# Another order of stages inside one step of a conv-mixer and mixture-of-experts kernel

## The reference, cut to what matters

```python
gating, index = jax.lax.top_k(affinity, k)
x_in = jnp.take_along_axis(x[:, None, :, :], index[..., None], axis=2)
h = jax.nn.gelu(jnp.einsum('bekd,edh->bekh', x_in, w1) + b1[None, :, None, :])
x_e = jnp.einsum('bekh,ehd->bekd', h, w2) + b2[None, :, None, :]
out = out.at[jnp.arange(Bx)[:, None], idx_flat].add(vals_flat)
```

## Time and profile before

| | us |
|---|---|
| median of three executions | 2999.71 |
| lowest, highest | 2988.85, 3001.3 |
| the profiled execution, its own time | 3005.34 |
| span of its instructions | 3002.5 |
| PE busy in it | 2067.5 (69%) |
| DVE busy | 1884.6 (63%) |
| ACT busy | 1360.2 (45%) |
| POOL busy | 1953.0 (65%) |

### The profile page before, as it was taken

One profiled execution on the slowest core, in us unless ns is written; L12 is line 12 of the kernel. 1 busy time (PEld: TensorE's weight loads), 2 busy tenths in 40 slices (PEclk: granted clock), 3 DMA queues, 4 the chain that ended last, 5 costly groups with the idle time before them and its releaser, 6 DMA issues.

```text
span 3002.5 us, 38138 instructions
## 1 busy us (share of the span) xinstructions
PE 2067.5 (69%) x11080; PEld 1164.1 (39%) x11080; DVE 1884.6 (63%) x4664; ACT 1360.2 (45%) x2308; POOL 1953.0 (65%) x1551
## 2 busy tenths in 40 slices
PE   3676777767777678777777777777777878744342
PEld 1233334343434344444434343444434443433221
DVE  1467686768677675858586776758675876753000
ACT  1334354554546454545545464545545364523210
POOL 0000256868777767778686767777686777777774
PEclk8877689898889887888889898888888797955555
DMA  4030415362534426263625435262625353334332
GB/s 114 10 81 0 115 22 131 46 148 36 119 76 93 106 44 147 42 152 46 148 35 119 74 76 117 44 152 44 149 41 135 51 107 73 71 63 79 40 61 50
DMA packets 284643, 244.66 MB, mean 81 GB/s; under 512 B 52368, under 2 KB 251264, under 8 KB 282112
## 3 DMA queue, kind: packets, MB, share of 16 engines
q0 software_dynamic: 110592, 80.31, 21.0%
q1 hardware_dynamic: 173824, 161.62, 18.7%
HBM read 83.71 MB, written 99.09 MB: 61 GB/s over the span
## 4 chain that ended last, share of the span: by engine, by line
PE 27%; issue 19%; POOL 16%; DVE 13%; ACT 10%; DMA 8%; SPq 6%; POOLq 0%; DVEq 0%; ACTq 0%
PE psum L1381 12%; POOL acc_dram L913 11%; POOL G L899 5%; PE psum L1407 5%; SPq L827 4%; DMA acc_dram<-Y,IDA 4%; DMA G<-rows_dram,IDX 3%; PE psum L1574 2%; ACT RS L935 2%; PE psum L1565 2%; PE psum L1417 2%; DVE hots L1277 2%; DVE XS L1189 2%; ACT RS L938 1%; PE psum L1487 1%
## 5 line engine op out<-in xcount | busy, mean ns | idle before, releaser
L913 POOL DMA_INDIRECT acc_dram<-Y,IDA x768 | 1163.2, 1515 | 446.0 <-issue 280.8
L899 POOL DMA_INDIRECT G<-rows_dram,IDX x768 | 784.2, 1021 | 578.5 <-issue 543.6
L1368 DVE TENSOR_TENSOR Y<-psum,GT 96x384 f32<-96x384 f32 x256 | 140.8, 550 | 450.4 <-PE psum L1574 390.4
L1277 DVE TENSOR_SCALAR_CACHE_REDUCE hots<-A,cand 96x384 f32<-96x384 f32 x720 | 401.6, 605 | 21.0 <-ACT A L1024 14.6
L1558 PE MATMUL psum<-m_all,G 96*128 96x96 f32 x768 | 130.9, 286 | 277.8 <-DMA G<-rows_dram,IDX 246.6
L1040 ACT ACTIVATE XG<-psum 128x288 f32<-128x288 f32 x256 | 103.7, 405 | 481.4 <-PE psum L1558 480.1
L1381 PE MATMUL psum<-U,m_all 128*128 128x384 f32 x576 | 266.9, 611 | 37.7 <-DVE DH L1133 28.0
L1574 PE MATMUL psum<-w2s,PH 128*96 128x128 f32 x1536 | 260.0, 316 | 0.0
L1381 PE MATMUL psum<-SQ,m_all 128*128 128x384 f32 x576 | 242.3, 549 | 20.3 <-DVE DU L1157 12.3
L1574 PEld LDWEIGHTS psum<-w2s,PH 128*96 128x96 f32 x1536 | 244.4, 198 | 14.6 <-issue 9.8
L1045 ACT ACTIVATE PH<-psum,b1s 128x288 f32<-128x288 f32 x256 | 127.8, 499 | 260.5 <-PE psum L1565 260.3
(11 more groups left out here) (170 smaller groups left out, 3905.2 us busy)
## 6 DMA issues: line engine op xcount, KB each, us to landing
stack<-XS SPq DMA_DIRECT2D x384, 100.0 KB
rows_dram<-XT SPq DMA_DIRECT2D x16, 1296.0 KB, 6.6
X<-in_x SPq DMA_DIRECT2D x16, 1152.0 KB, 5.7
acc_dram<-XT SPq DMA_DIRECT2D x16, 1152.0 KB
FT<-acc_dram SPq DMA_DIRECT2D x96, 192.0 KB, 3.1
out<-OT SPq DMA_DIRECT2D x96, 192.0 KB
G<-rows_dram,IDX POOLq DMA_INDIRECT x768
acc_dram<-Y,IDA POOLq DMA_INDIRECT x768
```

Source lines behind the costliest of these rows:

```text
L899: nc.gpsimd.indirect_dma_start(G[e % NG][:, c, :], None, rows_dram[of], bass.IndirectOffsetOnAxis(IDX[of][:, col:col + 1], 0)).then_inc(ga ...
L913: nc.gpsimd.indirect_dma_start(acc_dram, bass.IndirectOffsetOnAxis(IDA[of][:, col:col + 1], 0), Y[e % NY][:, c, :], None, compute_op=ALU.a ...
L1277: last = v.tensor_scalar((GT1, EQ1, P1)[i], A[:], cand[:, i + 1:i + 2].bitcast(F32), 0.0, ALU.is_ge, ALU.add, accum_out=cnt[:, i:i + 1])
L1368: v.tensor_tensor(Y[e % NY][:], bank6[0:CHUNK, 0:3 * C].rearrange("p (c n) -> p c n", c=3), GT[:, e % NH, :].unsqueeze(2).to_broadcast([CH ...
```

## The change

The list in `step` is put into another order; each engine therefore emits its stages in another order. One `tables()` call (an explicit load of the exp and ln table on ACT) is added. All other stages are the same, each as often as before. Because some stages now stand where an earlier wait no longer covers them, `fc1` and `fetch(1)` get waits of their own, and the SP stages raise the semaphore `sp_turn` after their waits.

The diff of the stages themselves, and the first lines of the diff of the list:

```diff
@@ step
     m.conv(s, 0, 0)
     q.lg_scale(s)
+    m.conv(s, 1, 0)
+    gather(2)
+    q.lg_shift(s)
+    layer2(0)
+    q.lg_exp(s)
+    m.conv(s, 0, 1)
...
@@ class Sync
             def load(self, b, par):
                 wait(sp, S["tokens_pe"], (b - 1) * TH)
+                sp.sem_inc(S["sp_turn"], 1)
                 sp.dma_start(X[par][:], x[b]).then_inc(x_loaded[par], 16)
...
                 if t == 0:
                     sp.wait_ge(S["xs"], done(b))
+                    sp.sem_inc(S["sp_turn"], 1)
...
             def store_acc(self, s):
                 sp.wait_ge(S["xt"], done(s))
+                sp.sem_inc(S["sp_turn"], 1)
...
             def store_slots(self, s, k):
 
                 sp.wait_ge(S["bank7_clear"], k)
+                sp.sem_inc(S["sp_turn"], 1)
...
                 wait(sp, S["slots_stored"], s * 16)
+                sp.sem_inc(S["sp_turn"], 1)
...
             def fetch(self, s, n, k):
 
-                if n == 0:
+                if n < 2:
                     wait(sp, S["acc_added"], (s - 2) * (48 * E))
-                elif n >= 2:
+                else:
                     sp.wait_ge(S["bank6_pe"], k)
+                sp.sem_inc(S["sp_turn"], 1)
...
             def put(self, s, n, k):
                 sp.wait_ge(S["bank6_clear"], k)
+                sp.sem_inc(S["sp_turn"], 1)
...
@@ class Tensor
             def fc1(self, s, par, k):
                 wait(pe, S["bank7_clear"], k - 1)
+                pe.wait_ge(S["xs"], done(s))
```

More of the change, by code:

```diff
@@ L333, in step @@
[L333 to L347, removed]
+    m.pre(s, 0)
+    decide(7)
+    q.count(s, 8, ka)
+    total(8)
+    q.ahead(s, 8)
+    turned(2)
+    m.z(s, par, 1, 1)
+    m.clamp(s, 0)
     decide(8)
+    m.z(s, par, 2, 0)
     turn(3)
-    m.pre(s, 0)
-    m.z(s, par, 1, 1)
+    tables()
@@ L427, in step @@
+    before(5)
+    m.scan(s, 2)
+    fetch(0)
+    q.ahead(s, 14)
+    m.hc(s, 1)
+    flip(1)
+    m.hc(s, 2)
     total(14)
-    m.decay(s, 2)
     decide(14)
-    m.yc(s, 0)
-    turned(5)
-    m.du(s, 2)
-    m.dbu(s, 2)
-    m.sq2(s, 0)
-    layer2(5)
-    weigh(5)
-    layer1(5)
-    q.above(s)
-    f.load(nxt, other)
-    before(5)
-    turn(6)
-    turned(6)
-    m.hc(s, 1)
-    m.spread_c(s, 2)
-    scatter(4)
-    gather(7)
+    flipped(1)
+    q.above(s)
+    m.var2(s, 0)
+    m.dpu(s, 1)
@@ L536, in step @@
+    f.xs(nxt, other, 0)
+    layer2(10)
+    m.mix_out(s, 1, last)
+    weigh(10)
+    layer1(9)
+    gather(12)
+    fetch(3)
+    before(9)
+    scatter(10)
+    m.xm(s, par, 0)
+    turn(10)
+    m.mix_out(s, 2, last)
+    m.xm_turned(s, par, 1)
+    m.xm_turned(s, par, 2)
+    turned(10)
+    gather(13)
+    m.xm(s, par, 1)
+    f.xs(nxt, other, 1)
+    flip(3)
+    q.hot(s, 2)
+    flipped(3)
+    layer1(10)
+    put(0)
     flip(2)
+    f.xs(nxt, other, 2)
     flipped(2)
-    f.var1(nxt, 2)
@@ new lines, in step @@
+    weigh(12)
+    layer1(12)
+    layer2(14)
+    tables()
+    m.rstd3(s, 1)
+    m.proj(s, 1)
+    m.rstd3(s, 2)
+    weigh(14)
+    put(3)
+    m.pr(s, 1)
+    scatter(12)
+    turn(13)
+    m.x2(s, par, 0)
+    fetch(5)
+    turned(13)
+    m.x2(s, par, 1)
+    before(12)
+    q.store_rows(s, par)
+    m.proj(s, 2)
+    m.tokens(s, par, 0)
+    flip(5)
+    flipped(5)
+    m.pr(s, 2)
+    m.tokens(s, par, 1)
+    m.xt(s, 0)
+    m.x2(s, par, 2)
+    q.store_slots(s, kg)
+    ks = q.bank7()
@@ L618, in step @@
+    q.slots_turn(s, ks)
+    m.stats(s, 0)
+    turn(14)
+    f.stack(nxt, other, 1)
     m.xt(s, 1)
     m.tokens(s, par, 2)
-    m.stats(s, 0)
+    turned(14)
+    q.columns(s, par, ks)
+    layer2(13)
+    m.stats(s, 1)
     f.stack(nxt, other, 2)
     gather(15)
-    m.stats(s, 1)
-    turned(13)
+    weigh(13)
+    layer1(14)
+    m.xt(s, 2)
+    m.store_acc(s)
+    m.stats(s, 2)
+    scatter(13)
     flip(4)
-    m.xt(s, 2)
-    m.stats(s, 2)
+    gather(16)
+    before(14)
+    m.moments(s)
@@ L628, in step @@
     flipped(4)
-    flip(3)
+    scatter(14)
     layer1(13)
-    flipped(3)
+    turn(15)
+    before(13)
+    put(4)
+    turned(15)
+    m.rstd4(s)
+    layer1(15)
+    before(15)
+    gather(17)
+    gelu(3)
     layer2(15)
     weigh(15)
-    put(4)
-    m.store_acc(s)
-    before(13)
-    layer1(12)
-    m.moments(s)
-    layer2(13)
-    weigh(13)
-    before(12)
-    ks = q.bank7()
-    q.slots_turn(s, ks)
-    q.columns(s, par, ks)
-    turn(14)
-    tables()
-    m.rstd4(s)
-    put(3)
@@ L649, in step @@
-    turned(14)
-    turn(15)
-    fetch(5)
-    layer1(14)
-    turned(15)
-    scatter(13)
-    before(14)
-    f.stack(nxt, other, 1)
-    flip(5)
-    layer1(15)
-    gather(16)
-    flipped(5)
-    layer2(14)
-    before(15)
-    weigh(14)
-    scatter(14)
-    gelu(3)
     put(5)
-    gather(17)
     scatter(15)
```

441 lines of the change are left out of this document (207 added, 234 removed).

## The result

The changed kernel takes 2918.55 us in the median of four executions (2900.45 to 2919.23). By the means of the executions on either side that is 0.9712 of the kernel before, with a 95% interval of 0.9659 to 0.9766: 2.9% faster. The profiled execution took 2919.23, 86 us less than the 3005.34 of before. Forecast were 2908, from a gain of 92 on that execution. The sum came out near the mark, but by errors that cancel.

What follows compares the result with a forecast made beforehand. It took the step as a ring that only a shorter compute stretch, turn(7) to weigh(9), shortens. 14 steps times 6.0 is 84, plus 8 at the start: 92 us off 3005.3, 2908 as median; range 2825 to 3020.

Steps and rivals of the forecast that it cites:

- POOL's waits ahead of scatter(8) and scatter(9) gone: Sign that the forecast is right: these waits for Y, 3.0 and 6.5 us before, gone or under 2 us.
- PE's wait at turn(15): Sign late in the step: PE still waits there for gather(15), near 9 us, from 9.8 before.
- DVE's hole behind `columns`: Sign: DVE's idle stretch before its next weigh takes the moved work and falls from 14.9 to some 6 us.
- First arc: turn(7) to weigh(9), where compute leads: moving unneeded stages off it saves 6.0 us per step, bounds 3.7 and 9.5.
- hot(2), 3.7: DVE stage directly ahead of weigh(9), with overlap taken off: moved behind weigh(10), it saves 3.7 us per step.
- normalise(1), 1.6: DVE stage between weigh(8) and the stages behind it: moved behind weigh(10), it saves 1.6 us per step.
- Second and third arc: scatter(9) to turn(15), then to the next turn(7), where POOL leads: DVE's hole takes moved work; nothing added, 0.
- 84 us for the steps: Whole run: 14 steps with mixer and stream, each 6.0 us shorter.
- 8 us for the start: Heads of steps 1 and 2: stack(1) no longer behind `store_acc`, 4 us less PE wait at each.
- POOL's floor: Rival: all POOL's waits vanish, a step takes 152 us, 14 less, in total about 2805 us; chance 0.20.
- Waits 0, table loads 0: Added waits are old when reached; two more ACT table loads per step are covered: 0 each, loads 2.6 at worst.
- Slower by the slot table: Rival: `store_slots` right ahead of slots_turn makes PE stand 8.4 us there; about 3035 us, chance 0.17.

Runs made afterwards that it cites:

- run 3: The changed kernel with hot(2) alone moved back to directly ahead of weigh(9): 2876.53 us, ratio 0.9582 to the kernel before.
- run 2: The kernel before with hot(2) moved behind weigh(10) and normalise(1) moved to normalise(2), consumers left in place: 3095.7 us, ratio 1.0301.
- run 5: The kernel before with hot(2) behind weigh(10) and hot_scale(2), slots_pe(2), slots_sum(2) and store_slots moved along: 3187.79 us, ratio 1.0634.
- run 4: The kernel before with normalise(1) alone moved from behind weigh(8) to directly ahead of normalise(2): 3000.7 us, ratio 1.0014.
- run 1: The kernel before, in its old order, with only the added waits and sp_turn increments of the change: 3003.26 us, ratio 1.0013.

## Why the prediction was right, and where it wasn't

- **POOL's waits ahead of scatter(8) and scatter(9) gone: right.** Means over 12 steps went from 1.9 and 6.5 us to 0 and 0; POOL's wait for Y in two steps from 27.3 to 0.9, where 12 was forecast. The loop's step, 161.5 us, is near the 160 named as a sign. PE's wait at turn(15), forecast near 9, moved ahead: from 7.3 us there to 2.6, 3.4 and 1.4 at turn(13), turn(14) and turn(15). DVE's hole behind `columns` came down from 14.9 to 9.4 us in the steps shown (6.6 in the mean), forecast 6.
- **First arc, 6.0 us: right in kind, too small.** It got 10.3 us shorter, more than the upper bound of 9.5. Its terms fared differently. hot(2), 3.7: right; run 3 has it back at 3.6, and moving it in the order of before (runs 2 and 5) took 2 to 3 us off the arc and about as much off POOL's wait ahead of scatter(9). normalise(1), 1.6: nothing in the order of before, where run 4 is like run 1. The other 6.7 us came with the stages that left PE's path, at a higher clock. The forecast had counted those only as leave for DVE to go faster, not as gain; which of them it was, no run took apart.
- **Second and third arc, "nothing added" and 0: the step that failed.** The time outside the first arc grew by some 6 us per step, 3.4 behind weigh(9) and 2.8 ahead of turn(7). The forecast asked whether DVE had room there, and it had; but POOL leads on these arcs, and its own instructions got longer. Its waits fell by 125 us, more than the 84 of the sum, and its busy time took 77 back, a term that the sum didn't have. Run 3 prices hot(2)'s part: with it behind weigh(10) a step takes 161.2 us, with it on the arc 157.5. So moving hot(2), the largest term of the forecast, was a loss of 42 us in the new order.
- **84 us for the steps: too much.** A step went from 165.4 to 161.2, 4.2 instead of 6.0, as the difference of 10.3 and some 6; from the first gather to the last scatter 48 us.
- **8 us for the start: 37.** Steps 0 and 1 have no stream, so the shorter compute chain shows in full: the first `lg_scale` 15.7 us earlier, step 1 another 15.6 (148.0 to 132.4), the rest ahead of the first gather. Step 0 has no search and no `store_slots`, so the SP block isn't behind its part either; PE's waits for stacks at the heads of steps 1 and 2, where the 8 were looked for, fell from 14.2 to 4.5. PE's busy time is 6.3 us less in step 0 and 12.9 in step 1 (granted clock 0.85 from 0.76). These 29 us too few and the 36 too many of the line above cancelled; that the total is right is luck.
- **POOL's floor at 152 us per step: the rival was half right.** All waits for Y are gone and POOL bounds the kernel, but at 161. The floor had moved: longer instructions and waits for landings are in it. "For it: compute stretches that had no reason to be long get shorter" is what happened. Against it the forecast held 153 us for step 1; that is the length of the window it read, and from one `lg_scale` to the next the step took 148.0.
- **Waits 0, table loads 0: right.** Run 1, and in the changed kernel a load still ends where the next instruction starts:

```profile
1514.75 1.28 ACT L1059 ACT_TABLE_LOAD   x1
1516.05 1.16 ACT L1059 ACTIVATE PH<-PH 128x1152 f32<-128x1152 f32 x1
```

  The drain of 1.38 us that the Trainium skill (ScalarE: Activation LUTs, What ACT_TABLE_LOAD costs) adds to a switch shows in no row; ACT's busy time grew by 37.5 us, for 33 more loads of 1.28 us.
- **Slower by the slot table: fell**, with 2.5 us once. Its sum has 6.8 us for the chain behind slots_sum(2) where its own terms give 6.6, which changes nothing.

## What to carry to other kernels

Cut the step at the marks that the forecast names and measure each stretch, in means over many steps: that showed that the first arc gained more than forecast and that the arcs where POOL leads gave much of it back. When work is moved to where its own engine is idle, ask what it does to the engine that leads there: put two-operand and double-rate DVE work where POOL waits anyway. When a stage is moved, move its consumers or leave it. Run the kernel once without the suspected bound (here the indirect DMAs) to see how much a change is worth beneath it. And don't take a share of the chain, or two differences of the same size, for a cause: ask where in the step the one lies and where the other, and what the waits there add up to.
